# Who issues the eight transposes of the first batch: ACT's queue or SP's, in a fused attention and feed-forward block

## What is computed

```python
# fake_quant(x, s, z) = (clip(round(x / s + z), 0, 255) - z) * s
x = x + tanh(g_xattn[0]) * matmul(fake_quant(layernorm(x), s1, z1), fake_quant(ctx, s2, z2))
# ffn: rows quantized to 8 bits by their own maximum, weights to -1, 0, 1
s = 127 / max(abs(x'), axis=-1);  xq = clip(round(x' * s), -128, 127) / s    # x' = layernorm(x)
scale_w = 1 / mean(abs(weight));  tw = clip(round(weight * scale_w), -1, 1)
x = x + tanh(g_ffn[0]) * einsum("bsi,oi->bso", xq, tw) / scale_w
```

## Time and profile before

| What | Value |
|---|---|
| median of three executions | 541.33 us |
| profiled execution, span | 541.5 us |
| PE busy | 462.7 us, 85% |
| DVE busy | 310.7 us, 57% |
| ACT busy | 213.6 us, 39% |
| POOL busy | 148.7 us, 27% |
| DMA moved | 105.06 MB, mean 194 GB/s |

### The profile page before, as it was taken

How to read it: one execution, slowest core, us unless ns; L and a number is a source line. 1 busy time by engine, 2 the same in 40 slices (tenths; PEclk the granted TensorE clock), 3 DMA queues, 4 the chain that set the end, 5 groups by cost and what they waited for, 6 DMA issues and landing times.

```text
span 541.5 us, 8629 instructions
## 1 busy us (share of the span) xinstructions
PE 462.7 (85%) x2048; PEld 203.4 (38%) x2048; DVE 310.7 (57%) x616; ACT 213.6 (39%) x219; POOL 148.7 (27%) x108
## 2 busy tenths in 40 slices
PE   0056777989988499999999887999999999999996
PEld 0022233434433144444444333444444444444442
DVE  2364766633288889734529659964499993222221
ACT  1733302648698664644503334255154662000000
POOL 1434535036011442538700403046023130000000
PEclk9997797998999889999999999999999999999999
DMA  6899999988889564999989999526012125122222
GB/s 197 247 284 255 300 182 294 336 289 275 275 273 245 97 105 125 250 353 354 291 300 287 278 318 278 182 77 235 0 20 56 22 40 179 74 77 77 77 77 77
DMA packets 87698, 105.06 MB, mean 194 GB/s; under 512 B 54656, under 2 KB 54656, under 8 KB 87680
## 3 DMA queue, kind: packets, MB, share of 16 engines
q1 hardware_dynamic: 69920, 100.68, 61.5%
q10 hardware_dynamic: 17760, 4.20, 6.2%
HBM read 75.50 MB, written 16.78 MB: 170 GB/s over the span
## 4 chain that ended last, share of the span: by engine, by line
PE 42%; DMA 20%; issue 14%; DVE 12%; POOL 8%; ACT 3%; SPq 1%; POOLq 0%; ACTq 0%; DVEq 0%
PE acc L743 27%; PE acc L730 15%; DMA turned_i<-tile_i 9%; POOL tile_i L384 5%; DMA ring<-in_ctx 4%; POOL ctx_i L407 4%; DMA ring<-in_L_ffn_weight 3%; DVE smalls L788 3%; DMA out<-h 1%; DVE lhs L835 1%; DVE h L851 1%; ACT tile_i L532 1%; DVE smalls L854 1%; DMA h<-in_x 1%; DMA ctx_i<-tile_i 1%
## 5 line engine op out<-in xcount | busy, mean ns | idle before, releaser
L730 PE MATMUL acc<-q,lhs 128*128 x1024 | 238.3, 394 | 62.7 <-DVE lhs L835 41.5
L743 PE MATMUL acc<-tw,lhs 128*128 x1024 | 224.6, 381 | 12.0 <-ACT tw L604 7.3
L730 PEld LDWEIGHTS acc<-q,lhs 128*128 x1024 | 102.8, 100 | 197.6 <-issue 92.5
L743 PEld LDWEIGHTS acc<-tw,lhs 128*128 x1024 | 100.6, 98 | 135.8 <-issue 18.3
L407 POOL TENSOR_SCALAR ctx_i<-ring,smalls 128x1024 int8<-128x1024 f32 x60 | 78.1, 1305 | 142.6 <-DMA ring<-in_ctx 119.7
L865 DVE SCALAR_TENSOR_TENSOR h<-acc,smalls,h 128x512 f32<-128x512 f32 x64 | 47.3, 748 | 82.9 <-PE acc L743 82.3
L512 ACT ACTIVATE q<-ctx_i 128x1024 bf16<-128x1024 int8 x64 | 64.6, 1049 | 51.3 <-POOL ctx_i L407 34.6
L384 POOL TENSOR_SCALAR tile_i<-h,smalls 128x2048 int8<-128x2048 f32 x24 | 50.2, 2090 | 120.3 <-DVE smalls L829 99.0
L851 DVE SCALAR_TENSOR_TENSOR h<-acc,smalls,h 128x512 f32<-128x512 f32 x64 | 47.7, 745 | 41.4 <-PE acc L730 40.7
L788 DVE BATCH_NORM_STATS2 smalls<-h 128x6 f32<-128x512 f32 x64 | 39.5, 680 | 11.0 <-DMA h<-in_x 10.8
L854 DVE BATCH_NORM_STATS2 smalls<-h 128x6 f32<-128x512 f32 x64 | 44.4, 694 | 2.2
(11 more groups left out here) (53 smaller groups left out, 121.5 us busy)
## 6 DMA issues: line engine op xcount, KB each, us to landing
ring<-in_ctx SPq DMA_DIRECT2D x64, 512.0 KB, 5.9
h<-in_x SPq DMA_DIRECT2D x30, 512.0 KB, 6.7
ring<-in_L_ffn_weight SPq DMA_DIRECT2D x24, 512.0 KB, 6.1
tw<-in_L_ffn_weight SPq DMA_DIRECT2D x16, 512.0 KB, 6.0
out<-h SPq DMA_DIRECT2D x16, 512.0 KB, 5.9
out<-h SPq DMA_DIRECT2D x32, 256.0 KB, 2.5
q<-in_L_ffn_weight SPq DMA_DIRECT2D x8, 512.0 KB, 5.4
h<-in_x SPq DMA_DIRECT2D x4, 256.0 KB, 5.0
```

Of the source, the lines that this page charges most:

```text
L730: done = nc.tensor.matmul(acc[j][:, :], flat(lhs[:, bass.ds(m, 1), k, :]), flat(q2[:, bass.ds(cc, 1), k, :]), start=(k == 0), stop=(k == K ...
L743: done = nc.tensor.matmul(acc[j][:, :], flat(lhs[:, bass.ds(m, 1), k, :]), flat(tw[:, bass.ds(pair * 2 + cc, 1), k, :]), start=(k == 0), s ...
```

## The change

The eight transposes of batch 0's x are taken out of ACT's list and put into SP's, between the loads. The loads keep their order among themselves. The transposes for x tiles 0, 1, 3, 4 and 5 follow the load of x 2, 3, 4, 5 and 6; that for x 2 stands between pieces 9 and 10; those for x 6 and x 7 follow the load of x 7. The rest of the program is as it was.

```diff
--- before.py
+++ after.py
@@ -306,12 +306,26 @@
 
             for c in range(C):
                 sp.dma_start(h[:, 0, c * NC:(c + 1) * NC], x_t[0][:, c * NC:(c + 1) * NC]).then_inc(x0_in[c], 16)
-            for m, first, end in ((1, 0, 2), (2, 2, 5), (3, 5, PIECES), (4, PIECES, PIECES + NB)):
-                load_pieces(first, end)
+            load_pieces(0, 2)
+            load_x(0, 1)
+            load_pieces(2, 5)
+            load_x(0, 2)
+            turn(sp, turn_ln1(0, 0))
+            load_pieces(5, PIECES)
+            load_x(0, 3)
+            turn(sp, turn_ln1(0, 1))
+            load_pieces(PIECES, PIECES + 2)
+            turn(sp, turn_ln1(0, 2))
+            load_pieces(PIECES + 2, PIECES + NB)
+            load_x(0, NB)
+            turn(sp, turn_ln1(0, 3))
+            load_pieces(PIECES + NB, 2 * PIECES)
+            load_x(0, NB + 1)
+            turn(sp, turn_ln1(0, NB))
+            for m in range(NB + 2, M):
                 load_x(0, m)
-            load_pieces(PIECES + NB, 2 * PIECES)
-            for m in range(NB + 1, M):
-                load_x(0, m)
+                turn(sp, turn_ln1(0, m - 1))
+            turn(sp, turn_ln1(0, M - 1))
 
 
             load_pieces(2 * PIECES, 2 * PIECES + NB)
@@ -612,30 +626,23 @@
             ctx_bf(0)
             ctx_bf(1)
             ctx_quant(2)
-            turn(act, turn_ln1(0, 0))
             ctx_bf(2)
             deviation1(0, 1)
             ctx_bf(3)
             ctx_quant(4)
             ctx_bf(4)
-            turn(act, turn_ln1(0, 1))
             ctx_quant(6)
             deviation1(0, 2)
             ctx_pieces(5, PIECES)
-            turn(act, turn_ln1(0, 2))
             ctx_bf(8)
             deviation1(0, 3)
             ctx_pieces(9, 11)
-            turn(act, turn_ln1(0, 3))
             ctx_bf(11)
             deviation1(0, NB)
             ctx_pieces(12, 2 * PIECES)
-            turn(act, turn_ln1(0, NB))
             deviation1(0, NB + 1)
             for m in range(NB + 2, M):
                 deviation1(0, m)
-                turn(act, turn_ln1(0, m - 1))
-            turn(act, turn_ln1(0, M - 1))
 
             for t in range(HELD - 2):
                 held_sum(t)
```

## The result

The changed kernel took 552.93 us, median of four executions (550.1 to 558.0), against 541.25 us before (539.8 to 550.44): a ratio of 1.0235, 95% interval 1.0131 to 1.0339. In a second session it took 553.25 us (549.72 to 556.89) against 537.38, a ratio of 1.0341 (1.0242 to 1.044). The forecast of 546.5 us had the sign, and less than half of the size: +5.2 us foreseen, some +12 measured, with 552.93 at the upper end of the range. The first execution that was profiled took 558.0 us, with a span of 556.2 us. Medians and ranges in this document are of all executions, while the ratios leave out those over 1.5% above the fastest of their kernel, as are the executions behind the traces called "before, third", "T4, T5 later" and "behind loads in flight". Each run is compared with executions of the kernel before from its own session.

A forecast was written before the change was run, and what follows sets the result against it. PE, 85% busy, was taken as bound by a slackless chain from SP's loads at 80 us to its feed-forward start at 189. 541.5 + 5.2 for late P20 - 0.2 for smaller waits gave 546.5 us, range 538 to 553.

The forecast's parts named there:

- P20: SP's load of piece 20 of ctx; forecast to go out at 115.3 us against 110.10, 5.2 us late.
- PE's gain: PE reaches the second half of x 5 to 9 us earlier; forecast worth nothing as long as P20 is late.
- The holds: SP's waits for POOL's int8 tiles before transposes of x 4, 5 and 7; forecast to move P16 from 67.06 to 82.4.
- T4: Transpose of x 4 in batch 0; forecast issued at 58.8 us and landing at 62 to 66 instead of 77.1.
- T7: Transpose of x 7, the last of batch 0; forecast to go at L + 25.1 to 26.1 us.
- L: The moment P15 lands, from which the holds are added up; taken as 55.5 us, bounds 53 and 59.7.
- X7: SP's load of x tile 7; forecast issued at L + 11.3 us, before at L + 3.4, landing at L + 17.4.
- P16: SP's load of piece 16 of ctx; forecast to go out at L + 26.9 = 82.4 us, against 67.06 before.
- H0: SP's first load of held weight; forecast 6.2 us after P16, at 88.6 against 79.99, and 26.7 us before P20.
- What a transpose costs the stream: Slowing of SP's loads: 1.8 us per early transpose from ACT's queue, 0.55 from SP's; the first four save 5.0 us.
- P15: SP's load of piece 15 of ctx; landed at 59.69 us before, forecast at 55.5 after a 1.5 us hold.
- The third rival: ACT-queue transposes cost loads only their bytes, so SP's holds cost in full: P20 at 122.9, 554 us; chance 0.16 (above 550.5).

The follow-up runs named there:

- before, third: The kernel before, unchanged, executed again for a third trace; session median 538.19 us (533.35 to 546.1).
- T4, T5 later: Changed kernel with the transposes of x 4 and x 5 each one load later, those of x 6 and x 7 still ahead of P16; 548.22 us, ratio 1.0217.
- behind loads in flight: Changed kernel with the transposes of x 4 to x 7 later among SP's loads, each int8 tile ready or nearly; 539.75 us, ratio 0.986 to the kernel before.

## Why the prediction was right or wrong

**What bounds the kernel: right.** The forecast took the stretch from P20 to the first feed-forward matmul for a chain without slack. In fourteen traces it is 78.8 to 81.7 us long, while P20 itself moves by 20 us. The mean granted clock of these traces goes from 0.948 to 0.981, and the length of the stretch does not follow it. PE's gain ahead of it was worth nothing, as forecast: PE waited 9.67 us for q.

**The holds: right in kind.** The run with the waits and no transpose in SP's queue lost all of it, and the run with only T4 to T7 moved did too. Step by step, L was 56.7 (55.5 forecast), X7 went out at L + 11.9 (11.3), landed at L + 17.4 (17.4), T7 was issued at L + 26.1 (25.1 to 26.1), P16 at L + 27.4 (26.9). P16 to H0 took 6.7 us (6.2) and H0 to P20 27.3 (26.7). PE's start at 78.17 (77.5) and T4's landing at 63.1 (62 to 66) were met. The sum for P20 was short by 2.8 us in one trace and 2.0 in the other.

**The step that failed: "P20 goes out at 88.6 + 26.7 = 115.3, against 110.10: 5.2 us late".** The first number was nearly right. The second was one execution's, and a late one. Four fronts of the kernel before (three traces of it, and the version that differs only in batch 1) have P20 at 110.10, 102.57, 109.38 and 100.81, mean 105.7 (104.5 without the third). The two traces of the changed kernel have 117.7. So P20 comes 12.0 us later and not 5.2; of the 6.8 us between, 4.4 lie in the number compared with and 2.4 in the sum. These are means of four traces and of two. The 12.0 us are near the loss of time that was measured, 11.7 and 15.9 us in two sessions: inside the first interval (7 to 18 us) and just under the second (13 to 24 us).

What made the 110.10 late stood in the forecast's own rows. P16 to H0 took 12.9 us there, and 7.1, 9.4 and 6.9 us in the other three fronts. The forecast took 6.2 us for this step in the changed kernel and left the 12.9 in the kernel that it compared with. It had also seen T4's 13.9 us and the 168 GB/s beside it, without asking whether they come in every execution. In the five traces in which SP waits for T6's and T7's tiles ahead of P16, P20 is at 117.3 to 120.7: there the waits come in every execution, and no P20 near 102 was seen.

**The time that the sum starts from.** The forecast took the span of its trace, 541.5 us, for the time. In each of the thirteen other traces the span is 1.8 to 1.9 us shorter than the time of its execution. By this the traced execution of the kernel before took some 543.3 us (an estimate), 2 us above the median: once more a late one.

**What a transpose costs the stream: right in sign, too large, and from one trace.** The forecast had P15 land 3.5 to 5 us sooner, 4.2 as taken. It landed at 59.7, 57.9, 65.0, 60.6 and 57.5 with T0 to T3 in ACT's queue and no wait of SP's ahead of it, mean 60.1, and at 56.6 to 58.8 in the eight traces with them in SP's, mean 57.5. So 2.6 us, and less scatter. T0 in ACT's queue took anything from 7.8 to 15.6 us, and one trace gave a single number for it. "T4 and T5 are worse" rested on the 168 GB/s of one execution: the same 12 us ran at 318, 261 and 294 GB/s in the other three fronts. And the window of 54 to 66 us, which the forecast took as one without a transpose, has T4 in flight from 63.2.

**The Trainium skill's rule of turns between queues** ("DMA: Bandwidth & Descriptors", "Queues, rings and completion order") was set aside because of the 168 GB/s of the earlier trace rows. With 318 GB/s in the same stretch of the second trace this is no ground against it, and no run here isolates the rule. The third rival, built on it, decides where L stays above 59; L was 56.7 and 57.6. That its 554 us lie nearer to the 552.93 measured than the forecast is luck: it had P20 at 122.9, which came at 118.08, and compared it with the same late 110.10.

**The end: wrong.** "From there the same distance to the end" did not hold in that trace: 358.3 us behind the first feed-forward matmul instead of 352.4. The second trace of the same kernel has 350.8, so the change does not bring this in every execution; whether it makes it more frequent two traces cannot tell. With batch 1's transposes in SP's queue it was 347.2 and 345.7.

**Open.** What makes one transpose of ACT's queue take 5 us and another 15 beside the same loads was not found; the experiments only remove the situation. For batch 1 the queue and the moment of issue changed together, and no run separates them. How much each of T6 and T7 costs by itself was not tried.

## What to carry to other kernels

A wait put into the list that issues the loads delays all loads behind it; the transpose it guards is cheap there (3.0 to 3.1 us to land in the changed kernel), and can stand where its input is ready, or nearly, and loads are in flight. Before a difference of a few microseconds is forecast from one trace, ask which of its numbers an accident of that execution has set, and take a second trace of the kernel before. A step that the sum prices one way for the changed kernel and that stands in the trace of before at twice the price (here P16 to H0, 6.2 and 12.9 us) is where to look. Look at the spread of the executions too: here those of the kernel before spread over up to 26 us, five times the change that was forecast.

## What the hardware did that was not expected

A transpose of 0.26 MB from ACT's queue beside loads from SP's took up to 15.6 us to land at the start and up to 13.7 in batch 1, and the same one differed by a factor of two between executions (T0: 7.8 to 9.9 us in four traces, 15.1 and 15.6 in two). T0 in SP's queue, between the same loads, took 7.9 to 8.7 us in eight traces, and T4 to T7 in the changed kernel 3.0 to 3.1, with hardly a load in flight ahead of them. Where ACT's T4 took 13.9 us, a load of SP's beside it was slow too: P16 landed after 11.5 us, against 5.6 to 8.1 in the other three fronts.

Of the kernel before, 17 executions of one session spread over 26 us and twelve more over 13; of the kernel with all transposes of x in SP's queue six spread over 4 us, and with batch 1's alone there six over 7. Fewer executions spread less by themselves, so only part of the difference need be the kernel's.
